# Waits between short rows of GpSimd's indirect DMAs, in a two-layer decoder on one core

## The reference, cut to what matters

```
x = ln(x + retention(x))            layer 0: 8 heads, chunked decay
x = ln(x + cross_attention(x, ctx)) 16 heads, 77 keys
x = ln(x + moe0(x))                 64 experts (256->64->256), top 8, plus 2 shared experts (256->512->256)
x = ln(x + linear_attention(x))     layer 1: 64-wide memory, causal
x = ln(x + cross_attention(x, ctx))
x = ln(x + moe1(x))                 8 gated experts (256->512->256), top 2
```

## Time and profile before

| | |
|---|---|
| median of 3 runs | 2405.17 us (2404.66 to 2424.46) |
| profiled execution | 2425.71 us, span 2423.9 us |
| granted PE clock, mean | 0.84 of full |
| busy in the span | PE 1855.9, PEld 1448.9, DVE 1167.5, ACT 625.9, POOL 772.9 us |
| software DMA queue (POOL's) | 33024 packets, 92.32 MB |

### The profile page before, as it was taken

One profiled execution on the slowest core, in us unless ns is written; L12 is line 12 of the kernel. 1 busy time (PEld: TensorE's weight loads), 2 busy tenths in 40 slices (PEclk: granted clock), 3 DMA queues, 4 the chain that ended last, 5 costly groups with the idle time before them and its releaser, 6 DMA issues.

```text
span 2423.9 us, 49277 instructions
## 1 busy us (share of the span) xinstructions
PE 1855.9 (77%) x19787; PEld 1448.9 (60%) x19787; DVE 1167.5 (48%) x3042; ACT 625.9 (26%) x957; POOL 772.9 (32%) x899
## 2 busy tenths in 40 slices
PE   4897776865763599967677774698988749999995
PEld 2675554653642367744454453477767649999995
DVE  3564543543531224545654453556655543465654
ACT  0231221211211035533333332143333311111110
POOL 0113434335237400045655553412232220123223
PEclk9997976877767799977778886688888769999998
DMA  9222432423433677766676776321111032223322
GB/s 299 91 85 81 153 118 88 135 81 131 160 112 132 164 209 230 227 191 218 211 219 212 235 225 202 113 97 37 45 54 37 28 115 72 68 88 96 103 90 75
DMA packets 269647, 322.84 MB, mean 133 GB/s; under 512 B 25083, under 2 KB 245487, under 8 KB 268655
## 3 DMA queue, kind: packets, MB, share of 16 engines
q1 hardware_dynamic: 236399, 227.38, 29.7%
q0 software_dynamic: 33024, 92.32, 11.9%
HBM read 157.22 MB, written 162.40 MB: 132 GB/s over the span
## 4 chain that ended last, share of the span: by engine, by line
PE 61%; issue 11%; another core or an unknown queue 9%; DVE 6%; ACT 4%; DMA 3%; SPq 3%; POOL 2%; DVEq 1%; POOLq 0%; ACTq 0%
PE wide L2014 11%; PE d_yp L2026 5%; PE bank L1163 4%; PE wide L1148 4%; PE wide L1151 3%; PE wide L110 3%; PE wide L1675 3%; PE bank L1171 3%; PE e_yp L1686 3%; PE wide L127 2%; PE bank L983 2%; PE wide L1135 2%; ACT pt L634 2%; PE e_xp L1663 2%
## 5 line engine op out<-in xcount | busy, mean ns | idle before, releaser
L1391 POOL DMA_INDIRECT big<-results,slots x256 | 254.5, 994 | 348.1 <-DMA results<-e_y 174.4
L2014 PE MATMUL wide<-d_xt,d_ws 128*128 128x128 f32 x2272 | 279.1, 277 | 0.6 <-issue 0.6
L2014 PEld LDWEIGHTS wide<-d_xt,d_ws 128*128 128x128 f32 x2272 | 272.7, 193 | 4.5 <-issue 1.0
L826 DVE RECIPROCAL rden<-bank 128x256 f32<-128x256 f32 x64 | 112.3, 1754 | 202.7 <-PE bank L1163 175.3
L574 POOL DMA_INDIRECT lists<-big,slots x160 | 154.1, 963 | 108.0 <-DVE slots L918 59.7
L110 PE MATMUL wide<-shared_sx,shared_sw 128*128 128x512 f32 x256 | 141.0, 677 | 58.5 <-ACT shared_sh L118 56.7
L535 POOL TENSOR_TENSOR rs<-mv,eps 128x4 f32<-128x4 f32 x32 | 6.6, 205 | 527.8 <-DVE mv L683 527.8
L634 ACT ACTIVATE pt<-wide 77x2048 f32<-77x2048 f32 x64 | 119.9, 1873 | 195.1 <-PE wide L1151 194.1
L1675 PE MATMUL wide<-e_xt,e_w1s 128*64 128x128 f32 x1280 | 107.0, 298 | 74.6 <-issue 48.7
L127 PE MATMUL wide<-shared_sw,shared_sh 128*128 128x256 f32 x512 | 128.0, 391 | 26.3 <-issue 24.8
L127 PEld LDWEIGHTS wide<-shared_sw,shared_sh 128*128 128x128 f32 x512 | 100.9, 198 | 72.3 <-issue 57.7
(11 more groups left out here) (275 smaller groups left out, 3666.0 us busy)
## 6 DMA issues: line engine op xcount, KB each, us to landing
lists<-zero SPq DMA_DIRECT2D x20, 2048.0 KB, 14.8
e_x<-lists SPq DMA_DIRECT2D x80, 512.0 KB
results<-e_y SPq DMA_DIRECT2D x80, 512.0 KB
d_x<-lists SPq DMA_DIRECT2D x71, 128.0 KB
results<-d_y SPq DMA_DIRECT2D x71, 128.0 KB
e_w<-in_L_w SPq DMA_DIRECT2D x2, 4096.0 KB
x<-in_x SPq DMA_DIRECT2D x8, 512.0 KB, 5.8
shared_sw<-in_x_t SPq DMA_DIRECT2D x32, 128.0 KB, 3.2
```

The source lines that it names most:

```text
L826: step(nc.vector.reciprocal(rden[:, p % 2], ps[:, KC * P:]))
L1391: pool.indirect_dma_start(out=picked[:, c % NG, b, :], out_offset=None, in_=results[0:-(-PAGES_OF_STEP[s] // 4) * 4 * R0, :], in_offset=ba ...
L2014: ins = mm(out[T % 2][:, a * P:(a + 1) * P], ws[:, T % NW, n, c, a * P:(a + 1) * P], xt[:, T % 2, c], start=c == 0, stop=c == KC - 1)
```

## The change

Every long sequence of indirect DMAs on POOL is cut into rows: before the next row POOL waits on the semaphore that the DMAs of the former rows increment when they land. The puts of layer 0 become rows of 5 (part 0) and 3 (part 1), layer 1's rows of 4, the gathers rows of one group (4), and the last put rows of 4.

```diff
@@ attention_phase, layer 0
                     for b in range(NB):
+                        if b:
+                            landed = K0 * NB * (i // 3) + (5 * b if part_no == 0 else 5 * NB + (K0 - 5) * b)
+                            pool.wait_ge(scattered[i % 3], 16 * landed)
                         for k in range(0, 5) if part_no == 0 else range(5, K0):
                             pool.indirect_dma_start(
@@ attention_phase, layer 1
                     for b in range(NB):
+                        if b == 2:
+                            pool.wait_ge(scattered[i % 2], 16 * (NB * K1 * (i // 2) + b * K1))
                         for k in range(K1):
@@ feed_phase, gather(pool, c)
                 store(pool, s - 1)
+            if c:
+                pool.wait_ge(got[(c - 1) % NG], 16 * NB * ((c - 1) // NG + 1))
             if c >= NG:
                 pool.wait_ge(summed, c - NG + 1)
@@ feed_phase, last put
                 for k in range(K0):
+                    if k % 4 == 0 and b + k:
+                        pool.wait_ge(put, 16 * (b * K0 + k))
                     pool.indirect_dma_start(
```

## The result

| | before | change |
|---|---|---|
| median, 4 runs each | 2404.91 us (2398.18 to 2424.46) | 2331.84 us (2318.74 to 2346.17) |
| ratio, with its 95% interval | | 0.9685 (0.9601 to 0.9768) |
| profiled execution's span | 2423.9 us | 2323.7 us |

The change is 3.2% faster, 73 us; the forecast was 77 us, 2328. The two profiled spans differ by 100 us, since the profiled execution of before was 20 above its median; a later pair on one chip (experiments 9 and 10) differs by 75 us, and sizes are taken from that pair where it has them.

The account below looks back on a forecast made before the run. PE has 61% of the chain; 9%, about 218 us, are unexplained waits, laid to POOL's long DMA rows. Terms -40 - 9 - 28 - 3 + 3 = -77 us, off the median 2405.17, give 2328 us; range 2250 to 2412.

Parts of the forecast that it names:

- The step on which all rested: POOL's long rows of indirect DMAs cause the unexplained waits, 213 of 218 us located; waits for landings give time back.
- rival A: Waits are added and the stalls stay, outliving each landing: slower, 2481 us; chance 0.16.
- rival B: The stalls aren't the rows' doing and the waits fall into POOL's idle time: 2412 us; chance 0.08.
- C: Rival: relief as forecast, and POOL doesn't bound, with landings at 2.82 us: 2246 us; chance 0.18.
- Attention phase: Layer 0's rows of 12 puts become four rows of 3; nearly all six unexplained pieces come back: -40 us (-45 to 0).
- Handover: From the 44 puts to the feed phase: stall gone, the puts then decide, list loads at 870: -9 us (-27 to +33).
- Gathers: Feed phase: POOL becomes the bound, 7.75 us a group, 62 us a step instead of 66: -28 us (-91 to +59).
- the point where the phase becomes a draw: Feed phase: with landings averaging above 4.5 us, a step is longer than 66 us whatever becomes of the stalls.
- Rival D: Partial relief: attention phases relieved (-40), feed phase and handover a draw through landings of 4.5 us: 2368 us; chance 0.13.
- Layer 1: Points 4 and 5: rows of 8 cut to two of 4, -3 us (-5 to 0); one more wait inside its last put, +3.
- Two of the signs named beforehand: In the changed profile: no unexplained piece over 3 us in 250 to 700, and first gathers of steps 62 us apart.
- The rule of the Trainium skill: DMA engines go round queues packet by packet, so a long row shouldn't hold another queue; the sum would be rival B's.

Follow-up runs that it names:

- experiment 9: The kernel before, unchanged, run again on chip 6: 2406.88 us.
- experiment 10: The change, unchanged, run again on chip 6: 2334.42 us, ratio 0.9685 to the kernel before; its section estimates 2186 us for the change on chip 9.
- experiment 1: The kernel before with waits only in layer 0's puts (rows of 5 and 3), on chip 1: 2358.32 us, ratio 0.9764.
- experiment 3: The change without the seven waits in the last 32 puts, on chip 1: 2332.81 us, ratio 0.968 to the kernel before.
- experiment 4: The change with a wait before every second group of gathers (rows of 8), on chip 1: 2301.00 us, ratio 0.9538 to the kernel before.
- experiment 2: The kernel before with only the change's waits in the gathers, on chip 1: 2408.83 us, ratio 0.9997.
- experiment 11: The change with each gather group waiting for the group before the last, on chip 3: 2328.84 us, ratio 0.969 to the kernel before.
- experiment 12: The change with gathers in rows of 8, puts of 10 and 6, last put in rows of 8, on chip 3: 2318.91 us, ratio 0.9616 to before.
- experiment 6: The change with each gather group waiting for the group before the last, on chip 9: 2068.52 us, ratio 1.0363 to the kernel before.
- experiment 7: The change without the waits between gathers, on chip 9: 2064.55 us, ratio 1.033 to the kernel before.
- the window: The change with each gather group waiting for the group before the last, at most 8 under way: 2068.52 us on chip 9, 2328.84 on chip 3.

## Why the prediction was right

The step on which all rested held, on the chips that have the stalls: the unexplained waits are the doing of POOL's long rows, and pauses take them away in the feed phase and shorten them in the attention phase. On chip 6 the first result repeated; on chip 9, where the stalls don't exist, the waits cost time. So rival A (the stalls stay) and rival B (the rows aren't the cause) are out, and so is C, by the pace that POOL sets. Point by point, with the pair on chip 6, 715.6/154.7/675.1/341.3 against 665.9/149.3/657.7/337.6:

1. *Attention phase*, -40: measured -50 (on chip 1, experiments 1, 3 and 4 against 2: -43 to -48). Under-sized, though the pieces weren't all gone: where the chain reaches back to the start, the unexplained time ahead of the 44 puts is 15, 20 and 27 us in experiments 1, 4 and 11, of 46 and 31 in the two profiles of before, with pieces of 4 to 5.5 us left in several steps and one of 13.4 in experiment 11. So at most 31 of the 50 us are pieces of the chain, and the rest came back elsewhere: PE's granted clock from 250 to 620 us was 0.79 before and 0.81 after, and PE did 4141 instead of 3581 matmuls in it. That this rest is stalls which PE's other work had covered is likely and not shown.
2. *Handover*, -9: measured -5 to -8. Its working held too: the puts decide now. From the first of the 44 to the first list loads it had 143 us (727.44 to 870); it was 145.3 (659.52 to 804.80), before 151.5. On chip 1 waits in the row of 44 gain some 17 us (H 136.6 in experiment 1 against 153.5 in 2), those in the last 32 give 9 to 12 back.
3. *Gathers*, -28: the mis-sized one. F gained 17 us on chip 6 and experiment 2's median nothing (0.9969 to 1.0025, so 7 us at most). A group takes 64.5/8 = 8.06 us, not 7.75: landing and wake-up are 4.3 us, just below the 4.5 us which the prediction had put as the point where the phase becomes a draw. Rival D, a draw in the feed phase, came half true. The stalls did go: ACT's waits of line 1558 from 120.5 to 6.0 us, and with rows of 8 the chain's unexplained share from 30.9% to 1.9% (the changed kernel's own chain doesn't reach so far back). In their place stands a new wait, DVE's 154.7 us for the gathers. Experiment 11 shows the draw: with the stalls left in and POOL waiting only for the group before the last, F is 652.7 us, with rows of 4 it is 652.9.
4. *Layer 1* (points 4 and 5), -3 and +3: measured -4 on chip 6, -7 over the means of the other runs (L 346.5 without its waits in experiments 1, 2 and before; 339.6 in 3, 4 and 12). The one more wait in each put costs less than the shorter rows give; the runs don't part the last put from the others.

Sum on chip 6: -50 - 5 - 17 - 4 = -76, of 75 us between the profiled spans (72 between the medians). A right sum with an attention term too small by 10 and a feed term too large by 11: the closeness is in good part luck. So is the chip: by the estimate of experiment 10, on chip 9 the same change would have been some 9% slower, a case that no rival had.

Two of the signs named beforehand failed. The granted clock of the feed phase did rise (0.79 to 0.85), and the first list loads moved behind the last put; but unexplained waits over 3 us are still there in the attention phase, and steps are 64.5 us apart, nearer to a draw's 66 than to 62.

The rule of the Trainium skill that spoke against the change, in "DMA: Bandwidth & Descriptors", section "Queues, rings and completion order", says that each DMA engine goes round the queues packet by packet. Chip 9 agrees with what the prediction drew from it: in the profiles of experiments 6 and 7 the chain has no unexplained wait. On chips 1, 3 and 6 something is held back, but the waits that grow are ACT's and DVE's on PE's signals, which that rule doesn't speak of; so no run here contradicts the rule, and it didn't bear on the question.

What do the rows hold back? This is the stall of the kernel before at 765 us, from the timelines of PE, POOL and ACT:

```profile
763.43 1.89 PE L127 MATMUL wide<-shared_sw,shared_sh 128*128 128x256 f32 x8
...
765.16 0.60 PE L1193 MATMUL bank<-ident,cw 128*64 128x128 f32 x4
...
782.15 0.96 POOL L574 DMA_INDIRECT lists<-big,slots  x1 [0.30 <-issue]
...
787.49 0.69 ACT L118 ACTIVATE shared_sh<-wide,shared_sb 128x512 f32<-128x512 f32 x1 [27.34 <-remote]
```

By its records PE had done its part by 766, and ACT went on only 5 us after POOL's last DMA was issued. The trace also has the times of nearly all semaphore increments, and these tell more. The increment for which ACT waited belongs to a matmul that ended at 763.60 by its record; it is there at 787.47, and ACT starts 0.02 us later. So ACT wasn't late: PE's signal was, by 23.9 us.

It is like this throughout. In the first profile of before, 113 of PE's 1180 recorded increments come more than 1.5 us after the end of the last matmul record that could have made them, by 24.1 us at most. In 112 of the 113 POOL issued indirect DMAs in that time or just before it (2 us). Of ACT's 577 and DVE's 1804 none is late, and in no other profile more than one. The late stretches of PE together cover 168 us ahead of quad 0 and 256 behind it up to the last gather; in the changed kernel 88 and 5 (on chip 6: 158 and 228, then 91 and 5), in the window 74 and 239, with gathers of 8 99 and 117, and in the four profiles on chip 9 none of some 1200 increments is late. So on the chips with stalls it is PE's semaphore increments that come late in POOL's rows, and of PE, ACT and DVE only PE's; in the attention phase they still do in the rows of 3 to 8 of the change.

What stays open is why. The end of a matmul's record is modelled, so whether the matmuls themselves were held or only their signals isn't shown; nor is why PE alone is hit, or why one chip of four is free of it.

## What to carry to other kernels

Where the chain has a large share that no event explains, set its pieces against each engine's timeline: here they lay in POOL's DMA rows. A pause of one landing every 8 gathers took all but 1.9% of the chain away; in the attention phase pauses every 3 to 5 puts took away some 50 us, and A is still 119 us longer on chip 3 than on chip 9 with the same program (663.0 against 543.8). A pause isn't free: work out the pace that it leaves to the issuing engine (issue times plus one landing a row), and make the row as long as the stalls allow; rows of 4 gave the gathers' gain back, rows of 8 kept 31 us more of it. And time such a remedy on several chips before it is kept: the change gained 3% where it was run twice, its relatives gained on two more chips, and on the fourth it would cost, by the estimate above, 9%.

## What the runs showed of the hardware that was not expected

- The same program, the kernel before, took 1996 us on chip 9 and 2407 to 2410 us on chips 1, 3 and 6. In the two profiles of the window (experiments 6 and 11) DVE is busy 1288.9 us on both chips and ACT 665 us, so the instructions aren't shorter. What differs are late increments of PE, the waits of ACT and DVE for them, and the clock (0.92 against 0.84 in the means of before's runs).
- On the chips with stalls PE's semaphore increments come late while POOL issues a long row, by up to 24.1 us in the first profile of before; those of ACT and DVE come on time.
- The ACT copies of the attention phase show it in one row. The change with puts of 10 on chip 9, then the change:

```profile
L639 ACT ACTIVATE pt<-wide 77x2048 f32<-77x2048 f32 x64 | 119.9, 1873 | 149.0 <-PE wide L1156 146.3
```

```profile
L639 ACT ACTIVATE pt<-wide 77x2048 f32<-77x2048 f32 x64 | 119.9, 1873 | 223.7 <-PE wide L1156 168.7
```

  The operation is equally long to the nanosecond, the idle time ahead of it 75 us longer. The rows of puts differ too, but in this the window, one program on both chips, agrees: 150.2 us on chip 9 and 223.8 on chip 3.
- How long a row may be differs by phase: rows of 8 gathers left 1.9% unexplained, puts of 10 and 6 (up to 16 in one row) cost 28 us against puts of 5 and 3 (up to 8).
- Indirect gathers of 128 KB follow each other every 1.26 us, and a row of 4 with its landing takes 8.06 us on a chip with stalls and on one without (64.5 us a step on both).
